# Attention of an eight-batch transformer layer: sums of probabilities on VectorE, halved ones products, and a new order on GpSimd and TensorE

## What is computed

```python
q, k, v = x @ Wq.T + bq, x @ Wk.T + bk, x @ Wv.T + bv      # 16 heads of 16
p = softmax(q @ k.T / sqrt(512))                            # over all keys
z = (p * triu(ones)) @ v
x = layernorm(x + (layernorm(x + z) * gamma + beta))
h = silu(x @ w1.T * s1) * (x @ w2.T * s2)                   # 256 -> 1024
h = gelu(h @ h1.T * s3);  h = gelu(h @ h2.T * s4)           # 1024 -> 1024
x = layernorm(x + h @ w3.T * s5)                            # 1024 -> 256
```

## Time and profile before

| | |
|---|---|
| median of 3 runs | 1321.23 us (1320.97 to 1322.27) |
| the profiled execution | 1322.63 us |
| its span on the core | 1320.6 us |
| TensorE busy | 1211.8 us, 92% of the span |
| VectorE busy | 812.8 us, 62% |
| GpSimd busy | 575.2 us, 44% |
| ScalarE busy | 528.4 us, 40% |

### The profile page before, as it was taken

One profiled execution on the slowest core, in us unless ns is written; L12 is line 12 of the kernel. 1 busy time (PEld: TensorE's weight loads), 2 busy tenths in 40 slices (PEclk: granted clock), 3 DMA queues, 4 the chain that ended last, 5 costly groups with the idle time before them and its releaser, 6 DMA issues.

```text
span 1320.6 us, 18260 instructions
## 1 busy us (share of the span) xinstructions
PE 1211.8 (92%) x7322; PEld 815.2 (62%) x7322; DVE 812.8 (62%) x1239; ACT 528.4 (40%) x698; POOL 575.2 (44%) x502
## 2 busy tenths in 40 slices
PE   4378999989999999998999999999999999999997
PEld 2144666647675576746666476754777466664886
DVE  5855486566755576566864667556775668655412
ACT  6775411554125531375115551165312751154311
POOL 5856432365225542365224552255422653245332
PEclk8578899999998999999999899989999999997999
DMA  9971433516234252245225063341523452341000
GB/s 328 277 179 44 159 66 66 122 26 191 65 82 97 81 142 63 54 98 169 60 61 130 18 191 66 76 103 52 154 63 72 98 164 60 66 106 26 1 0 16
DMA packets 55451, 128.48 MB, mean 97 GB/s; under 512 B 4032, under 2 KB 15680, under 8 KB 53312
## 3 DMA queue, kind: packets, MB, share of 16 engines
q1 hardware_dynamic: 51008, 115.44, 34.1%
q10 hardware_dynamic: 4352, 11.80, 2.8%
HBM read 88.95 MB, written 38.27 MB: 96 GB/s over the span
## 4 chain that ended last, share of the span: by engine, by line
PE 68%; issue 10%; POOL 9%; DVE 6%; DMA 4%; ACT 2%; SPq 1%; POOLq 0%; DVEq 0%; ACTq 0%
PE PS L977 45%; POOL diag_probs L437 6%; PE PS L862 5%; PE PS L894 5%; PE PS L831 4%; DVE neg_max L646 4%; PE PS L913 3%; PE PS L920 2%; DMA qk_rows<-qk_lo 2%; DMA stacks<-qk_rows 2%; POOL rstd L450 1%; PE PS L926 1%; PE PS L841 1%; ACT probsT L558 1%; PE PS L871 1%
## 5 line engine op out<-in xcount | busy, mean ns | idle before, releaser
L646 DVE TENSOR_REDUCE neg_max<-PS 128x2 f32<-128x1024 f32 x256 | 299.7, 1216 | 72.6 <-PE PS L862 72.6
L558 ACT ACTIVATE probsT<-PS 128x1024 f32<-128x1024 f32 x256 | 247.9, 1021 | 121.9 <-PE PS L894 121.9
L424 POOL TENSOR_TENSOR hidA_lo<-hidA_full,hidA_hi 128x512 fp32r<-128x512 f32 x128 | 165.0, 1289 | 265.2 <-DVE hidA_hi L793 194.6
L977 PE MATMUL PS<-hidA_hi,g 128*128 128x512 f32 x512 | 207.5, 405 | 0.0
L977 PE MATMUL PS<-hidC_hi,g 128*128 128x512 f32 x512 | 205.7, 402 | 0.0
L977 PE MATMUL PS<-hidA_lo,g 128*128 128x512 f32 x512 | 200.3, 391 | 0.0
L977 PE MATMUL PS<-hidC_lo,g 128*128 128x512 f32 x512 | 200.2, 391 | 0.0
L437 POOL TENSOR_TENSOR diag_probs<-probsT,mask 128x512 f32<-128x512 f32 x120 | 154.8, 1293 | 57.5 <-PE PS L977 31.0
L424 POOL TENSOR_TENSOR hidC_lo<-hidC_full,hidC_hi 128x512 fp32r<-128x512 f32 x64 | 82.2, 1284 | 218.8 <-DVE hidC_hi L793 218.8
L894 PE MATMUL PS<-stacks 66*128 66x512 f32 x512 | 162.3, 441 | 0.9 <-ACT probsT L558 0.4
L579 ACT ACTIVATE hidC_full<-PS,scales 128x512 f32<-128x512 f32 x64 | 44.1, 690 | 254.8 <-PE PS L977 254.8
(11 more groups left out here) (101 smaller groups left out, 1634.2 us busy)
## 6 DMA issues: line engine op xcount, KB each, us to landing
stacks<-qk_rows SPq DMA_DIRECT2D x64, 512.0 KB
stacks<-qk_rows SPq DMA_DIRECT2D x32, 1024.0 KB
qk_rows<-qk_hi SPq DMA_DIRECT2D x32, 512.0 KB, 3.7
qk_rows<-qk_lo SPq DMA_DIRECT2D x32, 512.0 KB, 5.3
xT_sb<-xT_dram SPq DMA_DIRECT2D x8, 512.0 KB, 4.1
raw_weights<-h1T_dram ACTq DMA_DIRECT2D x8, 512.0 KB, 10.4
raw_weights<-h2T_dram ACTq DMA_DIRECT2D x8, 512.0 KB, 9.1
x_tok<-x_dram SPq DMA_DIRECT2D x8, 512.0 KB, 5.5
```

Source lines behind the costliest of these rows:

```text
L424: nc.gpsimd.tensor_tensor(lo[:, m, :], full[:, m, :], hi[:, m, :], ALU.subtract).then_inc(lo_done, 1)
L558: nc.scalar.activation(PT[:, s % RING, 2 * pair:2 * pair + 2, :], PS[:, 2 * pair:2 * pair + 2, :], ACT.Exp, scale=SCALE).then_inc(exp_done, 1)
L646: nc.vector.tensor_reduce(NEGM[:, h // (H // 2), at:at + 2], PS[:, bank + 2 * side:bank + 2 * side + 2, :], AX.X, ALU.max, negate=True).th ...
L977: ins = nc.tensor.matmul(out, d if swapped else w, w if swapped else d, start=(k == 0 and part == 0), stop=(k == kts - 1 and part == 1))
```

## The change

1. VectorE adds the probabilities of key tiles 0 and 1 for the queries from 128 on, into a new buffer `PSUM` (probs_sum; it lies in SBUF), and then those of key tile 2 for the queries from 256 on (`add_probs`, two instructions for each of two tiles in each quad: 16 a batch). The ones products then take 128 columns of tile 0, 128 of the first sum, 256 of the second and 128 of tile 3: 640 columns in place of 1280. `values` waits for the sums at kt 1 and 2, and ScalarE waits for the first sum before it writes over the buffer of tile 0.
2. VectorE's order: the sums stand between the parts of `last_norm`, and those of quad g+1 around `take_z` of quad g.
3. GpSimd's order: `X_AT` goes from steps 4, 7, 8, 11 to 5, 8, 12, 13, each `rstd` comes one step later, and the first low part of Q comes before the last tile's first `rstd`.
4. TensorE's order: the four Q projection products go from behind the attention to between its last steps; behind the transpose of tiles 0 to 2 come K and two tiles of V, and behind the transpose of tile 3 two tiles of V in place of one. In the last batch the fillers go from 8, 32 and 4 to 4, 18 and 2.
5. `guard_v` becomes one pair of instructions over all of V, ahead of the first 1024x1024 layer, for which V is laid out without gaps (`VX` 272 in place of 288). `UNIT_AT` starts at step 4 in place of 2 and goes by 6 in place of 7, and the transposes of the maxima (`TURN_AT`) come at steps 54 and 108 in place of 58 and 116.

```diff
+ADDS = 4
-X_AT = (4, 7, 8, 11)
+X_AT = (5, 8, 12, 13)
...
+    PSUM = place("probs_sum", [P, QUAD, S - P], F32, A + 18 * KB)
...
-        UNIT_AT = {2 + 7 * u + 2 * (u // (UNITS // 2)): u for u in range(UNITS)}
-        TURN_AT = {58: 0, 116: 1}
+        UNIT_AT = {4 + 6 * u + 6 * (u // (UNITS // 2)): u for u in range(UNITS)}
+        TURN_AT = {54: 0, 108: 1}
...
-                    t, norm = divmod(s - (QT - 1 + LAG), QT)
+                    t, norm = divmod(s - (QT + LAG), QT)
...
+                if not last:
+                    split_qk(b + 1, range(0, 1))
                 rstd(b, QT - 1, 0)
                 if not last:
-                    split_qk(b + 1, range(0, 1))
+                    split_qk(b + 1, range(1, 2))
                 rstd(b, QT - 1, 1)
...
+                        if s >= RING and s % QT == 0:
+                            after(act, probs_added, b, ADDS * NQUAD, ADDS * (s // QT - 1) + 2)
...
+            def add_probs(b, s):
+
+                g, kt = divmod(s, QT)
+                lo = kt * P
+                if s == 1:
+                    after(dve, y_done, b, QT, 0)
+                elif kt == 1:
+                    after(dve, pv_done, b, STEPS, s - 2)
+                after(dve, probs_ready, b, STEPS, s + 1)
+                for pair in range(2):
+                    heads = slice(2 * pair, 2 * pair + 2)
+                    after(dve, exp_done, b, 2 * STEPS, 2 * s + pair + 1)
+                    total = PSUM[:, heads, lo - P:]
+                    if kt == 1:
+                        before = PT[:, (s - 1) % RING, heads, lo:]
+                    else:
+                        before = total
+                        after(dve, probs_added, b, ADDS * NQUAD, ADDS * g + pair + 1)
+                    nc.vector.tensor_tensor(total, before, PT[:, s % RING, heads, lo:], ALU.add).then_inc(probs_added, 1)
+
             def attention(b, first):
 
                 if not first:
-                    last_norm(b)
+                    last_norm(b, (0,))
+                add_probs(b, 1)
+                if not first:
+                    last_norm(b, (1,))
+                add_probs(b, 2)
+                if not first:
+                    last_norm(b, (2,))
                 for g in range(NQUAD):
+                    if g < NQUAD - 1:
+                        add_probs(b, QT * (g + 1) + 1)
                     take_z(b, g)
+                    if g < NQUAD - 1:
+                        add_probs(b, QT * (g + 1) + 2)
                     first_norm(b, g)
                     second_norm(b, g)
...
+                if not last:
+                    guard_v(b + 1)
                 for layer, full, hi in ((2, hidC_full, hidC_hi), (3, hidA_full, hidA_hi)):
...
-                        if not last and layer == 2 and m < QT:
-                            guard_v(b + 1, m)
...
+                if kt == 1 or kt == 2:
+                    after(pe, probs_added, b, ADDS * NQUAD, ADDS * g + 2 * kt)
                 for j in range(QUAD):
-                    nc.tensor.matmul(PS[32 * j:32 * j + 32, bank, lo:S], ONE[:, 0:32],
-                                     PT[:, s % RING, j, lo:S], start=(kt == 0), stop=False,
-                                     skip_group_check=True)
+                    if kt == 0:
+                        to, p = hi, PT[:, s % RING, j, 0:P]
+                    elif kt == 1:
+                        to, p = hi, PSUM[:, j, 0:P]
+                    elif kt == 2:
+                        to, p = S, PSUM[:, j, P:]
+                    else:
+                        to, p = S, PT[:, s % RING, j, lo:S]
+                    nc.tensor.matmul(PS[32 * j:32 * j + 32, bank, lo:to], ONE[:, 0:32], p,
+                                     start=(kt == 0), stop=False, skip_group_check=True)
...
-                for s in range(STEPS - LAG, STEPS):
-                    values(b, s)
+                if b < B - 1:
+                    project_half(b + 1, 0, 0)
+                values(b, STEPS - 2)
+                if b < B - 1:
+                    project_half(b + 1, 0, 1)
+                    project_half(b + 1, 1, 0)
+                values(b, STEPS - 1)
+                if b < B - 1:
+                    project_half(b + 1, 1, 1)
 
             def next_projections(b, last):
-                if not last:
-                    project(b + 1, range(DT))
+                if last:
+                    keep_warm(7, 4)
+                turn_x2(b, 0, last)
+                if not last:
+                    project(b + 1, range(DT, 2 * DT))
+                    project_v(b + 1, range(2))
                 else:
-                    keep_warm(7, 8)
-                turn_x2(b, 0, last)
-                if not last:
-                    project(b + 1, range(DT, 2 * DT))
-                    project_v(b + 1, range(QT - 1))
+                    keep_warm(7, 18)
+                turn_x2(b, 1, last)
+                if not last:
+                    project_v(b + 1, range(2, QT))
                 else:
-                    keep_warm(7, 32)
-                turn_x2(b, 1, last)
...
```

56 lines of the change are left out of this document (28 added, 28 removed).

## The result

The changed kernel takes **1352.23 us** (median of 4 runs, 1345.37 to 1361.55) against 1321.75 (4 runs) of the kernel before. The ratio is 1.0232, interval 1.0168 to 1.0296: 2.3% slower. Forecast were 1334 us, 12.6 above, and 1301 to 1356 as range: the sign and the range held, and the rise is 2.4 times the forecast one (30.5 for 12.6). The profiled execution took 1353.43 with a span of 1351.4; that of before had 1320.6, so there are 30.8 us to place.

A forecast was written before the change was run, and what follows sets the result against it. TensorE bounds the feed-forward and sets attention's pace, with VectorE nearly as full; the adds make VectorE late. Six middle batches +18.7, last -2.3, first -3.8: +12.6 on 1322.6 is 1335.2, median 1334 us, range 1301 to 1356.

The forecast's parts named there:

- The blocked adds: VectorE in attention: one add in each of quads 1 to 3 loses 0.8 us to GpSimd's masks, 2.4 us a batch.
- masks and tokens: GpSimd at the tokens' arrival: one more mask ahead of the wait, load some 2 us later; the two counted as nothing.
- The tail: From last tokens to feed-forward: 2.3 us in place of 3.4, a gain of 1.1 a batch.
- The clock: TensorE's granted clock: more and shorter waits, falls slow the projections; 1 us a batch, between 0 and 5.15.
- The rival with 5.15 in each batch: TensorE's clock falls in each batch, 5.15 us in place of 1.0: 1359 us; chance 0.18.
- The row maximum's wait: First 1024x1024 layer: TensorE's 0.73 us wait behind `guard_v` goes once `guard_v` stands ahead; -0.7 a batch.
- The last batch: Attention and tail of the last batch: +1.7, and -4.0 from 18 fillers in place of 32; -2.3 us.
- The first: First batch, tokens' arrival to feed-forward: 45.5 us in place of 49.3, -3.8.
- TensorE's saved columns: Ones products in attention: 640 columns fewer a quad, 4.4 us a batch, counted as nothing because TensorE waits for sums.
- the adds fit: Rival: no add meets a mask and TensorE's clock stays up; 1309 us, faster; chance 0.26.
- TensorE keeps the pace: Rival: VectorE fits wholly into its waits, adds much shorter than 0.95; about 1275 us; chance 0.06.
- it comes out even: Rival: result between the forecast and the rival *the adds fit*, 1319 to 1324 us; chance 0.10.

The follow-up runs named there:

- experiment 4: As experiment 3, but each add replaced by a one-input row maximum over the same probabilities, result unused: 1298.45 us, 0.985.
- experiment 1: The changed kernel without the adds: full ones products, no waits for sums, both new orders and small parts kept: 1261.92 us, 0.954 of before.
- experiment 3: The changed kernel with its sums computed but not used: full ones products, TensorE waits for no sum, ScalarE does: 1331.61 us, 1.0083.
- experiment 6: The kernel before with GpSimd's order alone: additions of beta (`X_AT`) and each rstd later: 1264.76 us, 0.957.
- Experiment 8: The kernel of experiment 1 with `guard_v` moved behind the copy m = 5 of layer 3: 1252.49 us, 0.9475 of before.
- experiment 7: The kernel before with one part of GpSimd's order at a time: each rstd later 1295.16 us, 0.984; additions of beta later 1317.05 us, 0.999.

## Why the prediction was right, and where it was wrong

The sign and the range held, in part by luck. The sum for an undisturbed batch was nearly exact, 151.15 + 5.7 - 0.7 = 156.15 against the best batch's 156.73, but by errors that cancel: a gain of the orders that it left out against adds and waits for sums that cost more than it had.

- **The adds** were to take 13.1 us a batch when free, and take 4 x (1.81 + 1.28) = 12.4. The row with one input in PSUM was a good measure.
- **The blocked adds**, 2.4 us (0 to 4.8): VectorE spends (80.1 + 50.4) / 8 = 16.3 us a batch on them, 3.9 above the free ones. The mechanism was right (experiment 4 shows it: with one input the same instructions take 1.8 us a pair), its size was nearer to the upper bound. The prediction said nothing of the other side: the masks take 0.18 us longer each, in all 176.4 us in place of 154.8, 2.7 a batch on GpSimd.
- **The adds together** cost an undisturbed batch 8.7 us (experiments 1 and 3), of which 3.4 are the blocking (experiment 4). The forecast's 4.4 + 2.4 = 6.8 was worked out against the waits of the old order; against the new order, which it took for the same, it is 1.9 too little.
- **"I count the two as nothing", masks and tokens: this step failed.** GpSimd's new order takes 4.4 us off an undisturbed attention (52.5 to 48.1, experiment 6) and all of the clock's loss behind the first batch, 54 us in all. I had seen the waits of 1.96, 1.71 and 2.37 for `diag_probs` in the earlier trace rows, and named only the first as GpSimd's stand before the arrival; the 2.37 is the same one in another batch. The 1.71 comes in a like way, which I had not looked for: GpSimd waits at an rstd for VectorE's variance with the next mask queued behind it. In the kernel before, just ahead of the wait at 1062.70:

```profile
1060.87 0.55 POOL L450 TENSOR_TENSOR rstd<-var_plus_eps,minus_half 128x1 f32<-128x1 f32 x1 [1.23 <-DVE var_plus_eps L716]
1061.39 1.26 POOL L437 TENSOR_TENSOR diag_probs<-probsT,mask 128x512 f32<-128x512 f32 x1
```

The sum of the changed kernel's best attention is 52.5 - 4.0 (orders, experiment 1) + 8.7 (adds) + 0.9 (the rest, with the waits for sums) = 58.1, where the prediction had 52.5 + 5.7 = 58.2.

- **The tail**, -1.1 a batch: in the changed kernel the feed-forward starts 1.9 us behind the tokens (462.79 to 464.73) where 2.3 were forecast and 3.4 stood before. As a gain of TensorE's order it can't be seen: set beside experiment 6, experiment 1 has it cost an undisturbed attention at least what it saves.
- **The clock**, 1.0 us a batch (0 to 5.15): measured (955.3 - 6 x 156.73) / 6 = 2.5 above the best batch. The sentence that waits of 1.96 and 1.71 "cost no clock" was taken as if shorter waits were safe: in the batch at 943.60 the 18 us at half clock stand behind one of 0.77. The 1.5 us too few are 9 of the 18 us that the forecast lacks. The rival with 5.15 in each batch overshot.
- **The row maximum's wait**, -0.7 a batch, became +0.3 (1.04 for 0.73): `guard_v` in one piece of 2.33 us (and 0.95 for its first instruction) stands ahead of the row maximum that TensorE waits for. "The new place is hidden by the first weight tiles" was the failed premise. Experiment 8 moved it and gained 9 us. The layer is 1.0 above its forecast; the best batch in all is 0.6 above, 3.5 of the 18 us.
- **The last batch**, -2.3, measured +2.1: the tail went as worked out (tokens at 1260.23 to the feed-forward at 1261.85 is 1.6, forecast 1.4), but the attention before it took 59.1 us, at a mean clock of 0.74 and with waits for sums of 1.79 and 1.96; how much of it is clock no run tells. These are 4.4 of the 18. **The first**, -3.8, measured -1.6: the other 2.2. From the first use of the tokens to the feed-forward it took 42.9 us (105.87 to 148.78), less than the 45.5 of the forecast. But VectorE came to that use 4.75 us later than the 101.12 of the earlier trace rows, behind two pairs of adds, and the forecast had left this at nothing. (The four shares, 9, 3.5, 4.4 and 2.2, come to 19; 0.8 of it goes off, since the forecast took 924.25 for the six batches before and not 925.0.)
- **TensorE's saved columns** show in no batch as a gain, as forecast, though no run has them without the waits for the sums. The last transposes wait for VectorE (1.44 and 1.31), as the step on the tail had it.
- Of the rivals, *the adds fit* is out (3.9 blocked, clock lost), and so are *TensorE keeps the pace* and *it comes out even*. Of what the profile was to show, the adds' 0.9 and 0.64 us and near 2, the vanished 1.26, the waits of 1 to 2 us for sums and the short tail are there; the layer's wait is not gone.

Left open: what makes the clock fall in one of two batches with the same waits. That the falls behind the first batch stop when the long waits for masks and sums are gone is shown (experiments 1, 6, 8), but experiment 4 kept its clock too in the six middle batches, though TensorE's ones products had 32.4 us of idle time before them over the execution, 24.8 of it for masks, and each of these attentions has five waits of 0.8 to 1.4 us. The split of the 20 us for the sums between waiting and clock is worked out from the best batches, not measured by a run of its own. And the gain of the small parts (the places of the row scores, the first low part of Q) has no run apart from TensorE's order.

## What to carry to other kernels

Before adding work to an engine that looks 7 us idle, look at what the in-order engines queue behind a wait on it: here the free gain (4%) was in moving GpSimd's rstd and additions by one to four steps, with no work changed, and a saving of TensorE columns that VectorE had to pay for lost more than it gave. Run each part of a compound change alone: the orders gained 60 us, the adds then lost 90, and the net hid both. Run the parts together too, where one wait can take another's place: 24 and 3 us apart were 54 together. The best version keeps the orders, leaves the adds out and puts `guard_v` late.

## What the runs showed of the hardware

- A VectorE instruction with two inputs in SBUF and a GpSimd mask product hold each other up: 3.46 in place of 1.81 us for a pair of adds, 3.95 us for two masks of 1.28. With one input it stays at 1.80 at the same place (experiment 4). The pair and the two masks begin at 429.30 and 429.93 and are through at 433.88, 4.6 us for 1.81 + 2 x 1.28 = 4.4 us of work: they take turns.
- TensorE's granted clock fell to 0.50 behind a wait of 2.19 us and one of 1.99, and not behind one of 2.08 (all in experiment 7 with the rstd later), and behind one of 0.77 in one batch of the changed kernel and not in another. No single length separates them.
- The Trainium skill (TensorE: Matmul & The Clock Gate, A second HAM failure mode: psum-queue depth-cycling) tells of another kernel whose clock oscillates since TensorE idles shortly and often between groups of matmuls. The changed kernel's trace fits that in kind: its clock falls in all eight attentions, and its longest wait in the best batch's is 1.58.
- Where the long waits were gone the clock was 1.00 in the seven attentions behind the first (experiments 1, 6 and 8). A lower clock did not always cost time: in experiment 3 attentions at 0.91, 0.97 and 1.00 all took 57.3 us.
